# Key/value projections that load four tiles ahead and mix their biases between products, and a window-attention stage whose first tiles are loaded and zeroed differently

## What is computed

```
# layer 0: attention in a window of 16 channels around each channel
q = Wq x + bq;  k = Wk ctx + bk;  v = Wv ctx + bv            # 128 x 128 weights, 1024 columns
x = x + tanh(g) * (Wo softmax(q . k_window / 4) v_window + bo)
# layer 0: quantised feed-forward, then layer 1: cross-attention whose
# keys and values are projections of the context, "interfered":
y = ctx W.T + bias;   y = y + 0.1 * amp * einsum(y, interference)
# layer 1: gated feed-forward with low-rank factors
```

## Time and profile before

| | |
|---|---|
| median of 3 runs | 3290.72 us (3285.51 to 3298.68) |
| the profiled execution | 3291.82 us, its span 3290.1 us |
| PE busy | 3107.4 us (94% of the span), in 20493 matmuls |
| DVE, ACT, POOL busy | 1852.3, 1053.5, 708.2 us |
| stage 1, stage 2 | 0 to 463.5 us, 463.5 to 846.0 us |
| granted TensorE clock, mean | 0.976 |

### The profile page before, as it was taken

One profiled execution on the slowest core, in us unless ns is written; L12 is line 12 of the kernel. 1 busy time (PEld: TensorE's weight loads), 2 busy tenths in 40 slices (PEclk: granted clock), 3 DMA queues, 4 the chain that ended last, 5 costly groups with the idle time before them and its releaser, 6 DMA issues. The chain is left out here.

```text
span 3290.1 us, 51992 instructions
## 1 busy us (share of the span) xinstructions
PE 3107.4 (94%) x20493; PEld 2362.6 (72%) x20493; DVE 1852.3 (56%) x2538; ACT 1053.5 (32%) x1555; POOL 708.2 (22%) x587
## 2 busy tenths in 40 slices
PE   7999979989599998999999899999999999999999
PEld 6788855655267785666666678887788888777876
DVE  3111138878688838777777578787666665200000
ACT  2222233332233326554555333333433333200000
POOL 0000020000000004333333355554344442000000
PEclk9999989999799999999999999999999999999999
DMA  5334347676522222222223544444554446643342
GB/s 181 125 114 141 116 140 134 154 184 117 205 71 78 71 97 108 83 86 92 92 92 113 165 156 156 156 156 155 189 164 155 155 159 214 213 149 119 121 143 99
DMA packets 370423, 445.61 MB, mean 135 GB/s; under 512 B 157488, under 2 KB 264624, under 8 KB 367296
## 3 DMA queue, kind: packets, MB, share of 16 engines
q1 hardware_dynamic: 354048, 394.04, 38.1%
q10 hardware_dynamic: 16192, 49.04, 4.1%
HBM read 257.69 MB, written 176.79 MB: 132 GB/s over the span
## 5 line engine op out<-in xcount | busy, mean ns | idle before, releaser
L2762 PE MATMUL g_ps<-g_xs,g_wq 128*128 128x512 f32 x2616 | 627.3, 393 | 0.0
L2762 PEld LDWEIGHTS g_ps<-g_xs,g_wq 128*128 128x128 f32 x2616 | 487.0, 189 | 99.9
L2846 PE MATMUL g_ps<-g_wd,g_h 128*128 128x512 f32 x1536 | 355.5, 392 | 0.0
L2846 PEld LDWEIGHTS g_ps<-g_wd,g_h 128*128 128x128 f32 x1536 | 290.4, 189 | 62.9 <-issue 1.1
L2275 POOL TENSOR_TENSOR g_wq<-g_s,g_wq 128x512 fp32r<-128x512 f32 x168 | 242.8, 1455 | 200.7 <-ACT g_wq L2340 200.7
L2275 POOL TENSOR_TENSOR g_wq<-fe_wt,g_wq 128x512 fp32r<-128x512 f32 x125 | 180.0, 1440 | 238.0 <-ACT g_wq L2336 238.0
L2704 DVE TENSOR_TENSOR g_ta<-g_ps,g_ta 128x1024 f32<-128x1024 f32 x4 | 4.9, 1224 | 375.8 <-PE g_ps L2843 375.8
L1369 PE MATMUL kv_gps<-kv_xh,kv_wh 128*128 128x512 f32 x512 | 205.5, 401 | 1.0 <-DVE kv_xl L1266 1.0
L1369 PE MATMUL kv_gps<-kv_xh,kv_wl 128*128 128x512 f32 x512 | 200.7, 392 | 0.0
L1369 PE MATMUL kv_gps<-kv_xl,kv_wh 128*128 128x512 f32 x512 | 200.7, 392 | 0.0
L1665 ACT COPY a_pt<-a_tps 128x1024 f32<-128x1024 f32 x128 | 129.4, 1011 | 205.6 <-PE a_tps L1821 205.3
(11 more groups left out here) (312 smaller groups left out, 5580.8 us busy)
## 6 DMA issues: line engine op xcount, KB each, us to landing
g_h<-g_hidden SPq DMA_DIRECT2D x176, 256.0 KB, 2.7
g_hidden<-g_h ACTq DMA_DIRECT2D x84, 512.0 KB, 3.6
fe_wt<-g_merged SPq DMA_DIRECT2D x43, 512.0 KB, 4.6
g_merged<-fe_wt SPq DMA_DIRECT2D x40, 512.0 KB, 3.6
kv<-kv_y SPq DMA_DIRECT2D x16, 1024.0 KB, 6.0
early_x<-x SPq DMA_DIRECT2D x32, 512.0 KB, 6.1
g_down<-fe_rows SPq DMA_DIRECT2D x22, 512.0 KB, 6.3
fe_wt<-g_down SPq DMA_DIRECT2D x22, 512.0 KB, 4.4
```

Source lines behind the costliest of these rows:

```text
L2762: w = pe.matmul(ps[:, bank(u, to), :], wq[q % NQ][:, l, P * k:P * k + P], xs[j][:, r, k, :], start=(first and k == 0 and a == 0), stop=(la ...
L2846: w = pe.matmul(to, tile[:, p % RING, l, cols], wd[f][:, r, os], start=(f == 0 and a == 0), stop=False)
```

## The change

Stage 1. Context tiles get four landing places: the two of before and two in the output buffer `y[:, 1]`, so load n waits for the turn of tile n-4. Tile 2 is turned into other banks of `gps`, and the even ones of the last four into `wps`; a turn waits only for the remainder of the tile before the last. SP starts with context tile 0, and the bias loads come behind tile 2. The factor loads of ACT come behind its first weight split. The biases are computed by 8 products with three columns each, in block 0's group c = 0 ahead of k = 4, into `wps`; ACT copies them after `high(1)`. The second weight mixing and what hangs on it (split, high and low part of the factors) moves from c = 2 to c = 3 of block 0. Of the 18 stack stores SP issues 9, ahead of its blocks; ACT issues the other 9 and no longer waits for them until `query_high(0)`.

Between the stages. x tile 0, the weights, biases, `bvr`, `g` and context tiles 0 and 1 of stage 2 lie where `wraw`, `wh[0]` and `wl[0]` of stage 1 lie, and SP issues their 13 loads in block 15 of stage 1, between `load_rounded(NK - 1)` and `store_query(NK - 1)`. The wait for the last projections' store moves from the end of stage 1 to the early loads in the middle of stage 2.

Stage 2. `power(0)` comes ahead of the masks on POOL; ACT clears one half of `kbd` and DVE the other, behind `norm(0)`; the two `vbd` are cleared by 26 memsets of 640 columns; PE waits for the masks at its first `turn` only, and ACT's first key for `c1` at 1.

```diff
@@ window_attention
+        reserved = s.sb("reserved", [P, 4 * D])
+        cond, w4, bias, bvr, g = (first[n] for n in ("cond", "w4", "bias", "bvr", "g"))
+        x = [first["x"], *(s.sb(f"x{i}", [P, D]) for i in range(1, XS))]
...
-                    sp.wait_ge(S["zv"], n + 1)
+                    sp.wait_ge(S["zv"], NJ // 5 * (n + 1))
...
-            load_x(0)
-            for i, w in enumerate((wq, wk, wv, wo)):
-                sp.dma_start(w4[:, i, :], w).then_inc(S["consts"], 16)
-            for i, w in enumerate((bq, bk, bv, bo)):
-                sp.dma_start(bias[:, i:i + 1], column(w)).then_inc(S["consts"], 16)
-            sp.dma_start(bvr[:, :], everywhere(bv, P)).then_inc(S["consts"], 16)
-            sp.dma_start(g[:, 0:1], everywhere(gates[0:1], P)).then_inc(S["consts"], 16)
-            load_cond(0)
             load_x(1)
-            load_cond(1)
             load_x(2)
...
-            sp.wait_ge(S["zk"], 1)
+            sp.wait_ge(S["zk"], 2)
...
                 if b == B // 2:
+                    sp.wait_ge(WE["kvout"], 16 * 2 * NK)
                     early_loads(sp)
...
             pool.wait_ge(S["xn"], 1)
             for i in range(2):
-                pool.memset(vbd[i][:, :, :], 0.0).then_inc(S["zv"], 1)
+                for j in range(0, NJ, 5):
+                    pool.memset(vbd[i][:, j:j + 5, :], 0.0).then_inc(S["zv"], 1)
...
-            act.copy(kbd[:, :, :], zero[:, 0:1].unsqueeze(2).to_broadcast([P, H, NJ * W])).then_inc(S["zk"], 1)
-            act.wait_ge(S["c1"], 5)
+            act.copy(kbd[:, 0:H // 2, :], zero[:, 0:1].unsqueeze(2).to_broadcast([P, H // 2, NJ * W])).then_inc(S["zk"], 1)
...
             stats(0)
             norm(0)
+            dve.memset(kbd[:, H // 2:H, :], 0.0).then_inc(S["zk"], 1)
...
             def turn(b):
+                if b == 0:
+                    pe.wait_ge(S["c1"], 5)
...
             pe.wait_ge(S["consts"], 16 * 10)
-            pe.wait_ge(S["c1"], 5)
@@ projections
+        xin = [x[:, 0, :], x[:, 1, :], y[:, 1, 0:D], y[:, 1, D:2 * D]]
...
-            return tps2[:, :] if n % 2 or n >= 12 else gps[:, 2:4, :].rearrange("p c n -> p (c n)")
+            if n % 2:
+                return tps2[:, :]
+            if n >= 12:
+                return wps[:, :, :].rearrange("p k n -> p (k n)")
+            return (gps[:, 0:2, :] if n == 2 else gps[:, 2:4, :]).rearrange("p c n -> p (c n)")
...
+            def load_x(n):
+                if n >= 4:
+                    sp.wait_ge(S["xt"], n - 3)
+                sp.dma_start(xin[n % 4], x_in[n]).then_inc(xld[n % 4], 16)
...
+            load_x(0)
             sp.dma_start(mt[:, :, :], mixing).then_inc(S["consts"], 16)
             sp.dma_start(am[:, 0:1], everywhere(amp, P)).then_inc(S["consts"], 16)
             load_x(1)
             load_w(0, 0)
+            load_x(2)
+            sp.dma_start(braw[:, 0:NB], bias).then_inc(S["braw"], 16)
+            sp.dma_start(braw[:, NB:NB + NK], bq).then_inc(S["braw"], 16)
+            load_x(3)
...
             sp.wait_ge(S["low"], 1)
+            store_stacks(sp, jobs[3:], starts[3:], widths[3:])
             every_block(sp, step)
...
             load_rounded(NK - 1, 1, w3)
+            sp.wait_ge(S["wp"], NB)
+            sp.wait_ge(S["g"], NC * (NB - 1))
+            sp.wait_ge(S["wl"], NB)
+            window_loads(sp)
             store_query(NK - 1)
...
             store(NB - 1, 1)
-            sp.wait_ge(S["out"], 16 * NB)
...
             act.wait_ge(S["low"], 1)
-            for (a, o, which), at, width in zip(jobs, starts, widths):
-                R = a.shape[0]
-                for i, part in enumerate(which):
-                    act.dma_start(flat(o[R * i:R * i + R, :]), parts[:, part, at:at + width].bitcast(F32)).then_inc(S["stacks"], 16)
-            act.wait_ge(S["stacks"], 16 * 3 * len(jobs))
+            store_stacks(act, jobs[:3], starts[:3], widths[:3])
...
                 if not isinstance(j, int) or j:
                     act.wait_ge(S["qst"], 16 * j)
+                else:
+                    act.wait_ge(S["stacks"], 16 * 3 * len(jobs))
...
             def turn(n):
-                pe.wait_ge(xld[n % 2], 16 * (n // 2) + 16)
-                if n >= 2:
-                    pe.wait_ge(S["xtl"], n - 1 if n < 13 else n)
+                pe.wait_ge(xld[n % 4], 16 * (n // 4) + 16)
+                if n > 2:
+                    pe.wait_ge(S["xtl"], n - 1)
+                if n == 12:
+                    pe.wait_ge(S["bm"], 1)
...
+            def biases():
+                pe.wait_ge(S["braw"], 32)
+                for k in range(NK):
+                    m = pe.matmul(bps.rearrange("p (a k) -> p k a", k=NK)[:, k, :], mix[:, k, :, :].rearrange("p g m -> p (g m)"),
+                                  braw[:, :].rearrange("p (a k) -> p k a", k=NK)[:, k, :], start=True, stop=True)
+                m.then_inc(S["bp"], 1)
...
-                        if c == 0:
-                            pe.wait_ge(S["bm"], 1)
-                        if c == 2:
+                        if c == 3:
                             weights(1, 1)
...
+                        if first and c == 0 and k == 4:
+                            biases()
@@ gated_decoder
+    def window_loads(sp):
+        sp.dma_start(first["x"][:, :], x[0]).then_inc(WE["xl0"], 16)
+        for i in range(4):
+            sp.dma_start(first["w4"][:, i, :], w["W" + "qkvo"[i]]).then_inc(WE["consts"], 16)
+            sp.dma_start(first["bias"][:, i:i + 1], column(w["b" + "qkvo"[i]])).then_inc(WE["consts"], 16)
+        sp.dma_start(first["bvr"][:, :], everywhere(w["bv"], P)).then_inc(WE["consts"], 16)
+        sp.dma_start(first["g"][:, 0:1], everywhere(a["g_xattn"][0:1], P)).then_inc(WE["consts"], 16)
+        for i in range(2):
+            sp.dma_start(first["cond"][:, i, :], cond[i]).then_inc(WE[f"cl{i}"], 16)
```

More of the change, by code:

```diff
@@ L52, in wait_apart, with window_attention @@
         eng.wait_ge(sem, value)
[L54 removed]
+def window_attention(nc, x_in, ctx_in, gates, x_out, early_loads, first, WE):
     H, W = 8, 16
@@ L211, in _, with power @@
             pool.wait_ge(S["c1"], 1)
+            def power(n):
+                pool.wait_ge(S["aggr"], 2 * n + 2)
+                pool.tensor_tensor(rstd[:, :], mv[:, 1:2], half[:, :], ALU.pow).then_inc(S["rstd"], 1)
+            power(0)
             def keep(out, in_, op, base, pattern, cm):
@@ L1005, in projections @@
         s = Scope(nc, ctx, tag)
+        x = s.sb("x", [P, 2, D])
+        y = s.sb("y", [P, 2, TOK])
+        first_at = -(-nc.sbuf_base // 32) * 32
+        wraw = [s.sb(f"wraw{i}", [P, D]) for i in range(2)]
+        wh, wl = [], []
+        for i in range(2):
+            wh.append(s.sb(f"wh{i}", [P, NK, P], F32R))
+            wl.append(s.sb(f"wl{i}", [P, NK, P], F32R))
+        first.update(window_tiles(nc, first_at))
         xh = s.sb("xh", [P, NK, TOK], F32R)
         xl = s.sb("xl", [P, NK, TOK], F32R)
-        wraw = [s.sb(f"wraw{i}", [P, D]) for i in range(2)]
-        wh = [s.sb(f"wh{i}", [P, NK, P], F32R) for i in range(2)]
-        wl = [s.sb(f"wl{i}", [P, NK, P], F32R) for i in range(2)]
-        x = s.sb("x", [P, 2, D])
-        y = s.sb("y", [P, 2, TOK])
         mt = s.sb("mt", [P, NK, M])
@@ L1060, in every_block, with store_stacks @@
             step(NB - 2, 0, NB - 3, NK - 2, w3)
+        def store_stacks(eng, jobs, starts, widths):
+            for (a, o, which), at, width in zip(jobs, starts, widths):
+                R = a.shape[0]
+                for i, part in enumerate(which):
+                    eng.dma_start(flat(o[R * i:R * i + R, :]), parts[:, part, at:at + width].bitcast(F32)).then_inc(S["stacks"], 16)
         def ready(eng, *waits):
@@ L1081, in _ @@
             load_x(0)
+            sp.dma_start(mt[:, :, :], mixing).then_inc(S["consts"], 16)
+            sp.dma_start(am[:, 0:1], everywhere(amp, P)).then_inc(S["consts"], 16)
             load_x(1)
             load_w(0, 0)
-            for n in range(2, 8):
-                load_x(n)
+            load_x(2)
+            sp.dma_start(braw[:, 0:NB], bias).then_inc(S["braw"], 16)
+            sp.dma_start(braw[:, NB:NB + NK], bq).then_inc(S["braw"], 16)
+            load_x(3)
             sp.wait_ge(S["wld"], 16)
             load_w(1, 1)
-            for n in range(8, B):
+            for n in range(4, B):
                 load_x(n)
@@ L1162, in _ @@
         def _(act):
-            for (a, _, _), at, width in zip(jobs, starts, widths):
-                act.dma_start(factors[:, at:at + width], flat(a)).then_inc(S["factors"], 16)
             def high(c):
@@ L1188, in _ @@
             weights(0, 0)
-            act.wait_ge(S["bp"], 1)
-            act.copy(bmix[:, :], bps).then_inc(S["bm"], 1)
-            act.wait_ge(S["bm"], 1)
+            for (a, _, _), at, width in zip(jobs, starts, widths):
+                act.dma_start(factors[:, at:at + width], flat(a)).then_inc(S["factors"], 16)
             for c in range(NC):
@@ L1194, in _ @@
```

(10 more changed lines are left out.)

69 lines of the change are left out of this document (32 added, 37 removed).

## The result

In five timed runs of each, taken side by side, the changed kernel has a median of 3270.99 us (3265.17 to 3275.30) and the kernel before 3297.67 (3285.51 to 3298.68): the ratio is 0.9933 [0.9919, 0.9946]. The last experiments timed both kernels again, with 0.9957 [0.9941, 0.9974]. The change is worth 0.4 to 0.7%. The forecast was 3261.0, a gain of 30.8; the time lies inside the range and 10 us above the forecast. The profiled run took 3272.41 and its span is 3270.7, 19.4 under the span before (3290.1).

What follows compares the result with a forecast made beforehand. PE was taken to bound stage 1, and only the head to count in stage 2; gains 7.0 + 6.7 + 7.7 + 4.7 + 4.7 = 30.8 took 3291.8 to 3261.0 us, range 3250 to 3275.

Steps and rivals of the forecast that it cites:

- Step 1: Way to block 0, stage 1: earlier tile loads start block 0 at 18.1 to 18.4; gain 7.0 us, ends 5 and 8.5.
- Step 2: Block 0 of stage 1: fewer waits, earlier loads and a better clock make it 39.7 us; gain 6.7 us.
- The first rival: PE's clock falls in the stop of about 3.5 us ahead of block 0; price 2.5 us, time 3263.5, chance 0.2.
- Step 3: Block 1 of stage 1: split stack stores leave PE a wait of 1.4 us; gain 7.7 us, ends 5 and 9.1.
- Step 4: End of stage 1: SP's wait for the last store moves away; gain 4.7 us, ends 4.0 and 5.0.
- Step 5: Head of stage 2: first select near 22 us instead of 25.2, plus 1.5 from the first beat; gain 4.7 us.
- the excess of the first beat: Stage 2's first beat, 2.7 us over the steady one from low clock and a late tile; 1.5 us taken back.
- the second: Rival, head of stage 2: POOL's zeros do not hold DVE back; 5.8 us more gain, time 3255, chance 0.12.
- The third: Rival: new waits at norm(1), the rounded weight and block 0's start eat 14.4 us; time 3275.4, chance 0.09.
- the slower one: Rival: moved tiles slow PE's reading for stage 1's 1536 products, 46 to 54 us; time 3307 to 3315, chance 0.01.

Runs made afterwards that it cites:

- second pair of traces: Fresh traces of the unedited kernel before (span 3295.1 us) and of the changed kernel, the latter's span 24.5 us shorter.
- run 6: Changed kernel with mask by compare, power(1) between the zeros' halves, biases in PE's stop before block 0, plus one needless 512-column product there; 3255.12 us.
- Run 8: Changed kernel, but ACT issues all 18 stack stores again and waits for their landing; 3286.24 us.
- run 9: Changed kernel with two landing places for context tiles and the old wait for the last projections' store at the end of stage 1; 3278.21 us.
- Run 2: Changed kernel, with POOL waiting for each of the 26 memsets to land before starting the next; 3276.71 us.
- run 3: Changed kernel, with DVE's mask operation made as a tensor_tensor compare with zero instead of a tensor_scalar; 3274.85 us.
- run 4: Changed kernel with the mask by compare, and POOL taking power(1) and waiting for norm(1) between the two halves of the zeros; 3263.63 us.
- run 10: The kernel before, unedited, traced and timed again; span 3295.1 us, median 3292.01 us over 11 runs.
- run 7: Changed kernel with the biases as 24 one-column products again, placed in PE's stop ahead of block 0; 3271.64 us.

## Why the forecast was right or wrong

- **Step 1, the way to block 0: 5.4 instead of 7.0** (6.7 in the second pair of traces). The chain was right, the landings were put 0 to 2 us too early: tile 0 at 4.6 as estimated, tile 1 at 8.25 instead of 6. PE then turned and mixed at the low rate up to 15. The lower end of 5 held.
- **Step 2, block 0: 6.5 instead of 6.7.** 39.86 us against a sum of 39.7. Three border waits of 1.0 and biases of 1.85 are as forecast. The first rival was given 0.2 and is real in more than half of the traces, at 1.3 to 2.8 us (I had 2.5). I had argued against it from the one stop in block 1, in which the clock held for over 3.5 us; that was an argument from one draw. That 39.86 came so near the sum is therefore in part luck: the profiled run was one in which the clock held. The Trainium skill (TensorE: Matmul & The Clock Gate, Why this matters for your kernels) advises against such pauses; of the eight traces with the stop of 3.49 us five agree and three do not, and in run 6 the clock fell behind one of 0.95 us.
- **Step 3, block 1: 8.3 instead of 7.7.** The wait left is 0.64, not 1.4. Run 8, which brings a wait of 9.18 back, shows that it is the split of the stores together with ACT's dropped wait; the two were not parted.
- **Step 4, the end of stage 1: 4.5 instead of 4.7.** From PE's last product to the new stage 2.5 us instead of 7.0; run 9 brings the wait of 4.5 back.
- **Step 5, the head of stage 2, is the step that failed: -0.7 instead of 4.7.** The sentence was "with memsets of some 0.6 us it waits at most that. It is off the path in the sum." The mask waited for all 26, and behind it stood the statistics of tile 1 and the bank of the values. Run 2 (gaps: 0.32 us) and run 3 (another form: 0.19 us) show the cause from two sides. With the mask free (run 3) the rest of the step nearly holds: first `select` at 22.4, where 22 was forecast; head 3.1 shorter than before, where 4.7 was; the excess of the first beat 1.6 less, where I took 1.5. So of the 5.4 missed here the mask has 3.8, and 1.6 lie elsewhere in the head, most of it between the first `select` and the turn of batch 0.
- **The other rivals.** The gain of the second (zeros that hold nobody back) did not come by itself, but run 4 had it, with the mask's new form and `power(1)` moved: a head 10.0 shorter than before, where I had put "up to 9 + 1.5". The third, at 3275.4, named the wrong mechanism but the right place. Nothing speaks for the slower one: the products of stage 1 stand 0.23 apart after as before.

Of the 11.4 us between the sum's 30.8 and the 19.4 of the spans, step 5 has 5.4 and stage 1 has 1.4. The remaining 4.6 lie behind the head, where no edit but the moved wait for the last projections' store acts, and within the scatter there (run 10). In the second pair of traces the part behind the head differs by 0.6 only, and 5.4 of the 6.3 us that are missing there are step 5. Whether a small part is a real effect stays open.

## What to carry to other kernels

An operation that one trace shows waiting beside another engine has no known bound: take as its upper end the whole run of back-to-back work of that engine, and ask what stands behind it on its own queue before it is called off the path. Cutting a long operation into pieces freed nobody here as long as the pieces followed each other without a gap; change the form of the waiting operation, or move the one instruction that others need between two pieces, and do both where two equal waits stand side by side, since each hides the gain of the other. And a single trace's lucky row (a clock that stayed up, a lock that opened) is a draw, to be forecast with its chance.

## What the runs showed that I had not expected

- A DVE `tensor_scalar` on 128x32 numbers took 11.90 to 11.93 us in five traces beside 26 memsets of POOL without a gap, 10.94, 12.56 and once 5.58 beside two long ones, and 0.32 with gaps between them; a `tensor_tensor` of the same size took 0.19 each time, a `tensor_scalar` on one column 0.15 to 0.16.
- The clock fell or held behind the same instructions, with a stop of 3.49 us in both cases, and it fell behind a stop of only 0.95 us, and at the end of 5.42 us of one-column products (run 7).
- DVE's memset of 4160 columns has a row of 3.52 us, but in every trace the engine shows 0.81 us of idle with nothing to wait for just ahead of it. From the end of `norm(0)` (442.31) to the next operation (446.57) it is 4.26, near the 4.5 of the forecast; which of the two is the memset's own time the trace does not tell.
- From the end of PE's last product to the first instruction of the next stage 2.5 us pass even where nobody waits for a transfer; ACT's last result and SP's last issue lie in the first 1.2 of them (to 437.54).
